# Narrower products on TensorE: weights multiplied with exchanged operands, halves packed side by side, an output projection in three rounded products, and another written-out order

## The reference, cut to what matters

```python
# layer 0, attention: 32 heads, low-rank queries and keys
q = rms_norm(h @ q_a_w, q_a_ln_w) @ q_b_w       # rank 192, per head 128 "nope" + 64 rotary
kv = rms_norm(c_kv, kv_a_ln_w) @ kv_b_w         # rank 64, per head 128 keys + 128 values
out = softmax(causal((q_pass @ k_pass.T + q_rot @ k_rot.T) * scale)) @ v @ o_w
...
# layer 0, cross step: similarities of the context with itself
Q, K = ctx @ Wq.T, ctx @ Wk.T                    # 64 features
sim = sum over heads of Q K.T; top 30% of a row kept, sigmoid, made symmetric, mixed with x
...
# layer 0, feed-forward: 7 routed experts (top 2) and a shared one
# layer 1, attention: 16 heads of 16
qkv = x @ Wqkv + bqkv
ctx = softmax(causal(rot(q) @ rot(k).T)) @ v
out = ctx @ Wout + bout
# layer 1, cross step
kv = context @ W_k.T + b_k
sim = (p @ kv) @ kv.T; layer norm, softmax, added to x
# layer 1, feed-forward: silu(x @ w_gate.T) * (x @ w_up.T) @ w_down.T, hidden 1024
```

## Time and profile before

| | |
|---|---|
| time, median of 3 runs | 683.64 us (682.92 to 683.88) |
| the profiled execution's own time | 685.0 us |
| its span, first to last instruction | 683.0 us |
| TensorE matmul busy | 662.7 us, 97% of the span |
| VectorE, ScalarE, GpSimd busy | 77%, 73%, 57% |
| mean granted TensorE clock | 0.996 of full speed |

### The profile page before, as it was taken

How to read it: one execution, slowest core, us unless ns; L and a number is a source line. 1 busy time by engine, 2 the same in 40 slices (tenths; PEclk the granted TensorE clock), 3 DMA queues, 4 the chain that set the end, 5 groups by cost and what they waited for, 6 DMA issues and landing times.

```text
span 683.0 us, 15811 instructions
## 1 busy us (share of the span) xinstructions
PE 662.7 (97%) x5382; PEld 567.8 (83%) x5382; DVE 526.2 (77%) x1687; ACT 498.0 (73%) x1288; POOL 390.5 (57%) x646
## 2 busy tenths in 40 slices
PE   8899999999999999999998999999999999999995
PEld 5678898989988898889977888889787887788785
DVE  2779987997999899766888855456798888748465
ACT  3889876878787776889876966665767786866633
POOL 2568746675485645688969555644872221535651
PEclk9999999999999999999999999999999999999999
DMA  9671105023040312230022011311020000011201
GB/s 300 163 227 33 32 2 139 17 55 102 21 136 17 100 42 48 62 94 18 1 94 63 1 46 47 90 51 47 0 94 4 4 3 3 3 47 48 93 1 61
DMA packets 34679, 41.20 MB, mean 60 GB/s; under 512 B 6748, under 2 KB 27494, under 8 KB 34600
## 3 DMA queue, kind: packets, MB, share of 16 engines
q1 hardware_dynamic: 34056, 39.87, 20.2%
q10 hardware_dynamic: 544, 0.33, 0.2%
HBM read 30.08 MB, written 1.05 MB: 46 GB/s over the span
## 4 chain that ended last, share of the span: by engine, by line
PE 82%; DVE 7%; POOL 6%; issue 2%; ACT 2%; DMA 1%; ACTq 0%; POOLq 0%; DVEq 0%
PE bank L1216 72%; PE bank L1230 8%; POOL stat L2426 2%; PE bank L1495 2%; DVE g_pair_lo L1954 1%; DVE bn L1977 1%; POOL probs L2426 1%; POOL probs L2423 1%; DMA w_down<-in_L_attn_kv_a_w 1%; POOL w_split_lo L2426 1%; POOL stat L2423 1%; DVE u_pair_lo L1954 1%; DVE y L1957 0%; DVE bilinear L1957 0%; ACT probs L1868 0%
## 5 line engine op out<-in xcount | busy, mean ns | idle before, releaser
L2423 POOL TENSOR_SCALAR probs<-probs,soft 128x256 f32<-128x256 f32 (+1 forms) x256 | 105.3, 432 | 62.3 <-DVE soft L2113 61.1
L1728 ACT ACTIVATE probs<-probs,soft 128x256 f32<-128x256 f32 (+1 forms) x256 | 113.3, 448 | 13.9 <-DVE soft L2105 13.4
L2426 POOL TENSOR_TENSOR w_split_lo<-w_raw,w_split_hi 128x512 fp32r<-128x512 f32 (+2 forms) x57 | 76.0, 1339 | 55.7 <-ACT w_split_hi L1629 51.5
L1216 PE MATMUL bank<-xT_hi,w_split_hi 128*128 128x512 f32 x256 | 103.8, 405 | 2.4 <-DVE xT_lo L1957 2.4
L1216 PE MATMUL bank<-xT_lo,w_split_hi 128*128 128x512 f32 x256 | 100.9, 394 | 0.0
L1216 PEld LDWEIGHTS bank<-keyT,qT 128*64 128x64 f32 x1024 | 72.6, 137 | 9.8 <-issue 5.9
L1216 PE MATMUL bank<-keyT,qT 128*64 128x256 f32 (+3 forms) x1024 | 79.8, 303 | 0.0
L2426 POOL TENSOR_TENSOR qT<-qT,xT_plain 64x512 f32<-64x512 f32 x44 | 56.7, 1288 | 36.4 <-DMA qT<-xT_plain 32.9
L1216 PE MATMUL bank<-xT_hi,w_split_lo 128*128 128x512 f32 x192 | 75.7, 394 | 0.0
L2105 DVE CUSTOM_DVE_ANT_0 probs<-bank,mask 128x128 f32<-128x128 f32 (+1 forms) x192 | 58.1, 332 | 14.9 <-PE bank L1216 13.9
L1629 ACT ACTIVATE qT<-bank 64x512 f32<-64x512 f32 (+1 forms) x80 | 47.1, 595 | 21.9 <-PE bank L1216 20.1
(11 more groups left out here) (253 smaller groups left out, 1865.0 us busy)
## 6 DMA issues: line engine op xcount, KB each, us to landing
qT<-xT_plain SPq DMA_DIRECT2D x88, 64.0 KB, 2.0
w_raw<-in_w_nopeT SPq DMA_DIRECT2D x8, 512.0 KB, 3.6
w_raw_heads<-in_w_o SPq DMA_DIRECT2D x8, 512.0 KB, 5.0
qT<-rope_buf SPq DMA_DIRECT2D x40, 64.0 KB, 2.0
w_raw<-in_w_gateT SPq DMA_DIRECT2D x8, 256.0 KB, 2.6
w_raw<-in_w_upT SPq DMA_DIRECT2D x8, 256.0 KB, 3.2
w_raw<-in_w_downT SPq DMA_DIRECT2D x8, 256.0 KB, 3.6
w_raw<-in_L_ffn_Wup SPq DMA_DIRECT2D x7, 256.0 KB, 2.6
```

What stands on the lines that cost most here:

```text
L1216: return t.matmul(out, lhsT, rhs, start=start, stop=stop, skip_group_check=shared)
L1728: ins = s.activation(p[:, at], p[:, at], ACT.Exp, bias=st[:, 0, r:r + 1], scale=-1.0, accum_out=st[:, 1, r:r + 1])
L2423: return g_.tensor_scalar(out, in0, s1, s2, op0, op1)
L2426: return g_.tensor_tensor(out, in0, in1, op)
```

## The change

- **Query weights.** "w_q g" is split. "w_k g" multiplies with exchanged operands: the 64 columns of `w_k_latT` are stationary and 192 columns of `w_nopeT` (no longer widened to 256) are streamed, 4 products per group, alternately to the lower and upper 64 partitions. ScalarE copies the result (`w_turned`, two copies), and "w_q g" turns it with 4 transposes. The load of a group is split into two, and the first part waits for "w_k" of two groups before instead of for all readers.
- **Context.** Wq and Wk are multiplied with each other first ("adj_w", 2 small products), and the result once with the context ("adj_qk"). The context lies as two halves on partitions 0-63 and 64-127, and the products of both halves go to the two halves of one bank ("adj_w", "adj_qk", "ctx_T") or to two banks in turn ("ctx_tok").
- **Second attention.** The value bias is left out of "v1" and added in the copy after "ctx1_T". This copy is now two rounded ones on ScalarE, and VectorE forms the remainders with two instructions; "out1" has 6 products of rounded parts per tile in place of 2 plain ones. `w_out1` is split into parts once, in "consts".
- **The end.** "out_norm 3" does the root of both tiles at once, and ScalarE takes these roots ahead of the norm of batch 2.
- **Order.** `PE_ORDER` and `ASIDE` are written anew; a ring "turned" of one buffer is added.

```diff
+            elif name == "w_k":
                 g, = k
                 nope, k_lat, _, _, _ = group_raw(g)
                 w.wait_ge(*raw_landed(g, 0))
-                out = wait_bank(("absorb", g))[:, :].rearrange("p (c h d) -> p c h d", c=2, h=GH)
+                out = wait_bank(("turned", g))
                 for i in range(GH):
-                    for c in range(2):
-                        ins = mm(out[:, c, i, :], nope[:, i, c * P:(c + 1) * P], k_lat[:, i, :])
+                    ins = mm(out[i % 2 * KVLR:(i % 2 + 1) * KVLR, i // 2 * QLR:(i // 2 + 1) * QLR],
+                             k_lat[:, i, :], nope[:, i, :], shared=True)
+                ins.then_inc(absorbed.sem, 1)
+            elif name == "w_q":
+                g, = k
+                w.wait_ge(*landed("identity"))
+                w.wait_ge(*abs_hi["w_k", g])
+                out = wait_bank(("absorb", g))
+                for c in range(2):
+                    for i in range(2):
+                        ins = transpose(out[:, (2 * c + i) * P:(2 * c + i + 1) * P], w_turned[:, i, c * P:(c + 1) * P])
                 ins.then_inc(absorbed.sem, 1)
...
+            elif name == "adj_w":
+                w.wait_ge(*landed("xattn"))
+                out = wait_bank(step)
+                for h in range(NHALF):
+                    ins = mm(out[ctx_rows(h), 0:CTX], w_qk_x[:, 0, :], w_qk_x[:, 1, :], shared=True)
+                ins.then_inc(adj_qk_ready.sem, 1)
             elif name == "adj_qk":
...
                 for h in range(NHALF):
-                    out = wait_bank(("adj_qk", i, h))[0:CTX, :]
-                    mm(out, w_qk_x[:, i, :], ctxT[:, h * HALF:(h + 1) * HALF]).then_inc(adj_qk_ready.sem, 1)
+                    ins = mm(out[ctx_rows(h), :], w_both_x[ctx_rows(h), :], ctxT[ctx_rows(h), :], shared=True)
+                ins.then_inc(adj_qk_ready.sem, 1)
...
-                for tile in range(NT):
-                    ins = mm(out[:, tile, :], ctxT[:, tile * P:(tile + 1) * P], w_kv_x[:, :])
+                outs = [wait_bank(("ctx_tok", h)) for h in range(NHALF)]
+                for i in range(TH):
+                    for h, out in enumerate(outs):
+                        ins = mm(out[:, i * CTX:(i + 1) * CTX], ctxT[ctx_rows(h), i * P:(i + 1) * P], w_kv_x[ctx_rows(h), :])
...
             elif name == "v1":
...
-                    mm(part, ones1[:, :], bias1[:, 2 * D:3 * D], i == 0, False, True)
...
             elif name == "out1":
...
-                        ins = mm(part, ctx1_T[:, c, i * P:(i + 1) * P], w_out1[:, c, :], False, c == DC - 1, True)
+                        ins = mm3(part, ctx1_T[:, c, i * P:(i + 1) * P], w_out1[:, c, :], False, c == DC - 1, True)
...
+            elif name == "w_k":
+                g, = k
+                w.wait_ge(*absorbed["w_k", g])
+                if g:
+                    w.wait_ge(*absorbed["w_q", g - 1])
+                out = bank_of(("turned", g))[:, 0:2 * QLR].rearrange("p (i q) -> p i q", i=2)
+                copy(w_turned[:, :, 0:QLR], out)
+                copy(w_turned[:, :, QLR:], out[:, :, P:]).then_inc(abs_hi.sem, 1)
...
-                copy(ctx1_T[:, :, :], bank_of(("ctx1_T", b))[:, :].rearrange("p (c s) -> p c s", s=S)
-                     ).then_inc(ctx1_T_copied.sem, 1)
+                w.wait_ge(*landed("attn1"))
+                for c in range(DC):
+                    ins = s.activation(ctx1_T.hi[:, c, :], bank_of(step)[:, c * S:(c + 1) * S], ACT.Identity, bias=v_bias[:, c:c + 1])
+                ins.then_inc(ctx1_T_copied.sem, 1)
...
+            elif name == "ctx1_T":
+                b, = k
+                w.wait_ge(*ctx1_T_copied[b,])
+                for c in range(DC):
+                    ins = stt(ctx1_T.lo[:, c, :], bank_of(step)[:, c * S:(c + 1) * S], v_bias[:, c:c + 1], plain(ctx1_T.hi[:, c, :]),
+                              ALU.add, ALU.subtract)
+                ins.then_inc(ctx1_T_lo.sem, 1)
...
+                quarter, r, half = (stat[place][:, j, 0:TB] for j in range(3))
+                w.wait_ge(*sqrt_taken["last", TB - 1])
+                own(root_of_quarter(quarter, half, r))
+                w.wait_ge(*own.now)
                 for i, t in enumerate(batch_tiles(b)):
-                    quarter, r, half = (stat[place][:, j, i:i + 1] for j in range(3))
-                    w.wait_ge(*sqrt_taken["last", i])
-                    own(root_of_quarter(quarter, half, r))
-                    w.wait_ge(*own.now)
-                    ts(x[:, t, :], y[:, t, :], bn[place][:, i, 6:7], r, ALU.subtract, ALU.mult).then_inc(last_normed.sem, 1)
+                    ts(x[:, t, :], y[:, t, :], bn[place][:, i, 6:7], r[:, i:i + 1], ALU.subtract,
+                       ALU.mult).then_inc(last_normed.sem, 1)
```

More of the change, by code:

```diff
@@ L216 @@
-ASIDE = {
-    ("adj_mask", 2, 0): 65, ("adj_mask", 2, 1): 172, ("att_mix", 3): -20, ("att_norm", 1): -34, ("att_norm", 2): -158,
-    ("ctx1_T", 2): 77, ("down_root", 1): -40, ("down_scale", 0): -74, ("f_split", 0, 4): -35, ("load", 1): 2,
-    ("load", "const"): 43, ("load", "identity"): -42, ("load", "xT1"): 42, ("norm", 3, 4, 1): 5, ("pv", 0, 7): -37,
-    ("q_lat", 1, 2, 1): -39, ("qk_split", 2, 1): 3, ("route_soft", 0): -82, ("s", 2, 7, 1): -58, ("s", 3, 0, 0): 14,
-    ("s", 3, 4, 1): -6, ("s", 3, 6, 0): 53, ("sim_mix", 2): -7, ("split", 13, 2): -90, ("split", 15, 2): -61,
-    ("st1", 0, 3, 0): 12, ("st1", 2, 1, 0): 19, ("st1", 3, 2, 0): 17, ("w_q", 3): -95, ("xT", "attn1", 3): 4,
+down 0, w_k 0, down 1, w_q 0, w_k 1, down_T 0, w_v 1, q 0 0 0, w_q 1, down_T 1, w_v 0, q 0 0 1, q 1 0 0, adj_w,
@@ L444, in make_plan @@
         before = [] if g < 2 else [s for part in unit_readers(g - 2) for s in part]
-        stage(("w_q", g), "PE 1.76, ACT 1.02, DVE 1.35, POOL 0.78", ("load", g), *before,
+        stage(("w_k", g), "PE:cols64 0.7, ACT 0.85", ("load", g, 0),
+              holds=[bank("turned", g, left=(("w_k", g), "ACT")), Hold("turned", (g,), By(("w_q", g), "PE"))])
+        stage(("w_q", g), "PE 0.47, ACT 1.02, DVE 1.35, POOL 0.78", ("w_k", g), ("load", "identity"), *before,
               holds=[bank("absorb", g, left=(("w_q", g), "DVE"))])
-        stage(("w_v", g), "PE:cols64 0.88, ACT 0.5, DVE 0.6", ("load", g), *before,
+        stage(("w_v", g), "PE:cols64 0.88, ACT 0.5, DVE 0.6", ("load", g, 1), *before,
               holds=[bank("vo", g, left=(("w_v", g), "DVE"))])
@@ L815, in write_program @@
     lowT_ready = signal("lowT_ready", keys("down_T", (0, 1, "key")))
-    absorbed = signal("absorbed", keys("w_q"))
+    absorbed = signal("absorbed", [s for s in ORDER["PE"] if s[0] in ("w_k", "w_q")])
     vo_ready = signal("vo_ready", keys("w_v"))
@@ L822, in write_program @@
     out_ready = signal("out_ready", keys("out"))
-    adj_qk_ready = signal("adj_qk_ready", keys("adj_qk", range(NHALF)))
+    adj_qk_ready = signal("adj_qk_ready", [s for s in ORDER["PE"] if s[0] in ("adj_w", "adj_qk")])
     sim_ready = signal("sim_ready", keys("adj_sim", range(TB)))
@@ L855, in write_program @@
     rot_hi = signal("rot_hi", keys("w_q"))
-    abs_hi = signal("abs_hi", keys("w_q"))
+    abs_hi = signal("abs_hi", [s for s in ORDER["ACT"] if s[0] in ("w_k", "w_q")])
     vo_hi = signal("vo_hi", keys("w_v"))
@@ L2666, in sync_program @@
                     load(n, small[n])
-                else:
-                    if n >= 2 and n - 2 < U_EXPERT:
-                        for read in (absorbed, vo_ready, rot_lo, rot_rest):
+                elif part == [1]:
+                    if n >= 2:
+                        w.wait_ge(*vo_ready[n - 2,])
+                    load_group(n, 1)
+                else:
+                    if 2 <= n < U_EXPERT + 2:
+                        w.wait_ge(*absorbed["w_k", n - 2])
+                        for read in (rot_lo, rot_rest):
                             w.wait_ge(*read[n - 2,])
```

300 lines of the change are left out of this document (171 added, 129 removed).

## The result

The changed kernel takes 677.4 us (median of 5 runs, 675.64 to 680.03), the kernel before 683.64 in the same runs (682.92 to 683.88). The ratio is 0.9915, with a 95% interval of 0.989 to 0.9941. The gain is 6.2 us where 10.2 were forecast. These two medians come from few runs: in all runs that were made later, the kernel before has a median of 684.27 (43 runs) and the changed one 676.7 (11 runs, these five among them), 7.6 us apart. The profiled execution of the changed kernel took 677.4 us, its span is 675.6; before it was 685.0 and 683.0.

The account below looks back on a forecast made before the run. TensorE was taken to bound the kernel (82% of the chain). 10.3 us saved there plus 0.9 at the end less 1.0 of stalls gave 10.2: profiled 685.0 to 674.8, median 683.64 to 673.4 us; range 669.5 to 678.

Parts of the forecast that it names:

- Query weights, 3.6 forecast: First attention: "w_k" at 0.77 plus transposes at 0.53 replace 1.82 us, saving 0.52 in each of 7 groups.
- Context, 4.3 forecast: Context steps: array halves run side by side, saving 2.5 us in "adj_qk", 0.9 in "ctx_T" and 0.9 in "ctx_tok".
- Rival 1: Context steps: quadrants of one bank do not run side by side, 2.2 us of gain missing, 675.6 us; chance 0.12.
- Second attention, 2.4 forecast: TensorE there: 1.0 us saved by dropping bias products from "v1", 1.4 by rounded products in "out1".
- 14 x 0.12: New "out1" group: 2 bias products and 12 of rounded parts at 0.12 us each, 1.7 us where it took 2.03.
- ScalarE's turn and VectorE's cover: First attention: ScalarE's added copies (6.4 us) and VectorE at 89% cost nothing, since neither is full and steps stand between.
- rival 4: First attention: "w_q" waits for ScalarE's copy of `w_turned`, slower than before, 689 us at 2 us a group; chance 0.04.
- rival 2: New order costs more: longer waits at stage changes, short ones behind VectorE, 4 to 5 us, about 678; chance 0.14.
- The cover for the 1.1 us before "out1": Last batch: the longer "ctx1_T" copy is hidden by "bi_kv 2", "xT ffn 1" and "bi_sim 2"; uncovered, 1.1 us once.
- The end, 0.9 forecast: Last tiles: roots ahead of the norm and one root chain, stores issued earlier, 0.9 us less; bounds 0.4 and 1.5.
- New stalls, 1.0 forecast: Whole kernel: the new order and fuller engines add waits, 0 to 6 us, taken as 1.0 against the gain.

Follow-up runs that it names:

- second profile of the changed kernel: Profile from running the changed kernel once more without any edit: its fastest run there; median 675.93 us, ratio 0.9892.
- start_turned_later: The changed kernel with "w_k 1" moved behind "down_T 0" at the start: 675.92 us, ratio 0.9885.
- the old order: The changed kernel with all its parts, but with TensorE's order and the table of shifts of the kernel before: 685.61 us, ratio 1.0023.
- before_fills: The kernel before with full products put into three of TensorE's waits: 684.26 us, ratio 1.0.
- fill_turns: The changed kernel with 10 repeated transposes in TensorE's wait at the start of the second attention: 676.07 us, ratio 0.9893.

## Why the prediction came out as it did

The median is inside the range (669.5 to 678.0), 4.0 us above the number. Faster was right, and so was the mechanism: shorter groups on TensorE's list, which bounds the kernel. Of the terms some were too small and some too large. By its own steps:

**Query weights, 3.6 forecast.** Over groups 1 to 7 the old "w_q" take 12.6 us from start to start, and in the second profile of the changed kernel "w_k" take 5.05 (0.65 to 0.80 each) and the transposes 3.4 (0.44 to 0.53): 4.2 saved. That group 0 saves nothing, because it stands ahead of a wait, was right. The first query product did come 1.5 to 1.7 us earlier than in the profile of before, but the product waits for VectorE's list behind the end of "down", and moving "down_T 0" ahead by 2 us did not move it (start_turned_later). Of the 1.7 us, 1.1 is spread between executions of the kernel before (25.74 and 24.65); the forecast had nothing for the rest, and what ends "down" earlier is open.

**Context, 4.3 forecast.** "adj_qk" saved 2.46 with 0.26 for "adj_w", "ctx_T" 0.86, "ctx_tok" 0.89: 4.2. Rival 1 is refuted: the first records of "adj_qk" of the two quadrants start 7 ns apart, each of 512 columns, and write one bank; the group of four records takes 1.00 us, where four after each other took 1.86.

The rule of the Trainium skill that was weighed (TensorEngine Tiling (Array Packing), Restrictions and Gotchas), that different row tiles cannot use one bank at the same time, does not agree with this trace, and the measurement decides: with one bank the two row halves took 1.00 us, not 1.86. In this kernel they write different halves of the bank's partitions; two row halves on the same partitions of one bank are in no run here.

**Second attention, 2.4 forecast, 0.75 measured.** The terms were nearly right: 1.0 for the bias products of "v1", 1.0 measured for "out1" where 1.4 stood: the four groups take 1.73, 1.76, 1.87 and 1.77 us where they took 2.03, 2.04, 2.15 and 1.88, so none reached the 1.68 of 14 x 0.12, and the last was short before. But the stretch got only 0.75 shorter. Waits did not take the rest: the new one of 0.8 for `k_rows` stands near the end, but the 1.4 for `g_pair_lo` at 639 us is gone, and over the stretch TensorE waits 2.5 us before and 2.6 in the second profile. Counted from start to start without waits, 16 narrow products of the cross step (`kvT,outT`) take 3.5 us where they took 2.5, and the 16 transposes of `top_rows` 2.8 where they took 2.2. Both stand among other neighbours in the new order. Why they cost more there is open: TensorE changes the shape of its products 66 times in this stretch and 63 times before, which is hardly more, and no run tested it.

**ScalarE's turn and VectorE's cover.** Right. No wait names `w_turned`, and rival 4 is refuted. From 26 us on no single wait of TensorE in the first attention is over 0.7 us, in either profile of the changed kernel. The short waits of rival 2 did appear, more of them behind GpSimd than behind VectorE, but in all they are 1.3 to 2.1 us and not its 4 to 5. The cover for the 1.1 us before "out1" was claimed to be the steps in between, and the price without them "the whole chain": the old order, with 1 to 3 steps there in place of 3 to 6, waits 4.8 us in three pieces.

**The end, 0.9 forecast.** 1.2.

**New stalls, 1.0 forecast.** This term was too small. Waits grew by 2.0 us in the first profile (12.7 to 14.7), part of them harmless, as that for the load. In the first attention, where before had none, they are 1.3 us there and 2.1 in the second profile (`probs` 0.8, `xT_lo` 0.7, `qT` 0.6). There the groups give 4.2 + 2.5 + 0.9 = 7.5 us, less 2.1 of waits, and the stretch got 5.2 shorter against before_fills: the account closes to 0.2. The forecast also put 4.6 of the old 12.7 us ahead of 26 us; with the wait for the load of `w_down`, 1.1, it is 5.6.

**What was missing** is a term between the sum and the median. The sum said 674.8 for the profiled execution and 673.4 for the median, and the fastest execution took 673.4; that this is so near is luck, since it sets the fastest of 11 against a profile above its median. Of the 4.0 us, 0.7 lie in the choice of runs of the changed kernel (677.4 against 676.7 for all 11) and 0.6 in those of the kernel before (683.64 against 684.27). Another 2.1 go when three waits are filled (674.57). About 0.5 is left for the terms: 10.2 forecast, 9.7 measured with fills, 9.3 profile against profile. Here too terms cancel, 0.6 too little for the query weights and 0.3 for the end against 0.4 too much for "out1" and the stalls.

The forecast took the clock as given, and every instruction as equally long in each execution. A stretch of 3.4 us at half clock behind the wait at 350 us costs 1.5 us (from the router to the first "qkT" it is 152.08 us in the profile of fill_turns, 150.54 without), the one of 6.8 us at 493 about as much by the difference above, and the late `kT` 1.2. The mean clocks of 0.985 to 0.997 say that most other executions have low stretches too. How the 2.1 us divide between the clock and the late `kT` no run shows.

The Trainium skill says of the clock gate that its window is free-running, so that the same kernel sees a different number of slow matmuls from run to run (TensorE: Matmul & The Clock Gate, part 1). The granted clock of the 11 runs of one program, between 0.985 and 0.997, agrees with it.

Also open: why the kernel before, with waits of 1.5 and 0.7 us at the same change of stage, doesn't fall to half clock there in its profile. Its own fills bring nothing, and that is all that the runs show.

## What to carry to other kernels

Here a sum of shortened groups on the engine that bounds the kernel held to a microsecond in ten, with each group costed from start to start and with some luck among the terms, but it is worth that only with an order that hides the added latency: the same parts gave 6 to 8 us with one order and nothing with another. Where a planner writes the other engines' lists from one engine's order, moving a step there moves its producers too, and a step given more time can come out later than it was needed. After any change that moves waits, look at the times and the granted clock of several executions: a spread that has grown from 4 us to 8 is a cost that one profile can hide. A few full products in the waits are worth a try, with a control beside them. And before two profiles are laid side by side, ask for each where it lies among the times of its kernel: here 2 of the 11 us between two profiles came from that.

## What the runs showed of the hardware

- Two 64 x 64 quadrants of the array (rows and columns 0 to 63, and 64 to 127) that write the two halves of one bank's partitions run side by side: records 7 ns apart, 4 records of 512 columns in 1.00 us against 1.86 one after the other.
- At this change of stage, waits of 1.4 and 0.9 us, 11 us apart, were followed by 6.8 us at 0.50 of the clock in one execution, and waits of 1.5 and 0.8 us by none in another of the same program.
- One and the same VectorE instruction (`stat<-bn`, 128x4) takes 0.35 to 0.45 us in eight profiles and 1.65 to 1.71 in six; where it is slow, the span is 1.2 us longer at full clock.
- Products that do nothing useful, put into waits that are there anyway, went with a median 1.4 to 2.1 us lower in the changed kernel (674.57 against 675.93 and 676.7) and with none in the kernel before (684.26 against 684.28).
